# A decoder layer on one core: other places for a rotation, a norm, weight splits and function tables, and an end in halves

## The reference

```
x = x + attention(layernorm(x))        # 16 heads of 32, rotated queries and keys, causal
x = x + cross(layernorm(x), ctx)       # query and key from ctx (512 x 256 per batch), 128 wide
x = x + ffn(layernorm(x))

attention:  q, k, v = split(x @ w_atten.T);  q, k = rope(q), rope(k)
            y = softmax(mask(q k^T / sqrt(32))) v;  return y @ w_proj.T
cross:      energy = (ctx Wq^T + bq)(ctx Wk^T + bk)^T;  return x @ softmax(energy)
ffn:        shared = (silu(x Ws_gate) * (x Ws_up)) Ws_down              # 704 hidden values
            scores = softmax(x W_router);  the two best of 8 experts for each token
            h_e = silu(x We_gate) * (x We_up);  y_e = h_e We_down       # 352 hidden values each
            return sum over the two of score * y_e + shared
```

## Time and profile before

| | us |
|---|---|
| median of three runs | 1010.27 |
| the profiled execution | 1009.63 |
| its span | 1007.6 |
| PE busy in the span | 964.9 (96%) |
| DVE busy | 617.5 (61%) |
| ACT busy | 488.5 (48%) |
| POOL busy | 209.2 (21%) |

### The profile page before, as it was taken

The page is one execution under the profiler, slowest core; times in us unless marked ns, Lnnn a source line. Parts: engine busy times, 40 slices in busy tenths (PEclk is TensorE's granted clock), DMA queues, the critical chain, the costliest instruction groups (busy, mean ns, idle before and its releaser), DMA issues.

```text
span 1007.6 us, 18136 instructions
## 1 busy us (share of the span) xinstructions
PE 964.9 (96%) x6106; PEld 767.1 (76%) x6106; DVE 617.5 (61%) x1625; ACT 488.5 (48%) x1278; POOL 209.2 (21%) x247
## 2 busy tenths in 40 slices
PE   8988899999999999998899999999999999999998
PEld 6457666766767676665667788899889989899997
DVE  5698777867877767768353666524443344434665
ACT  1478765756747566568723331334444344432221
POOL 3222212221112211120000002222232222303342
PEclk9999999999999999999999999999999999999999
DMA  9665854438444473466800211744534542515554
GB/s 242 113 98 74 157 107 64 63 53 244 104 63 64 64 233 65 59 121 206 275 22 21 93 44 53 263 153 166 162 100 140 168 150 85 160 51 157 170 187 144
DMA packets 69834, 124.91 MB, mean 124 GB/s; under 512 B 6336, under 2 KB 22720, under 8 KB 69760
## 3 DMA queue, kind: packets, MB, share of 16 engines
q1 hardware_dynamic: 63296, 104.81, 41.6%
q0 software_dynamic: 5600, 18.35, 6.3%
q10 hardware_dynamic: 864, 0.79, 0.6%
HBM read 70.19 MB, written 28.57 MB: 98 GB/s over the span
## 4 chain that ended last, share of the span: by engine, by line
PE 77%; DVE 11%; issue 3%; DMA 3%; ACT 2%; DVEq 1%; POOL 1%; ACTq 0%; SPq 0%
PE ps L1379 23%; PE ps L1389 12%; PE ps L1139 8%; PE ps L1288 5%; PE ps L1230 5%; PE ps L1191 5%; PE ps L1178 3%; PE ps L1214 3%; PE ps L1164 3%; DVE gu_lo L1703 3%; DMA ks<-rope_a 3%; PE ps L1397 2%; PE ps L1250 2%; PE ps L1080 2%; DVE probs L1552 1%
## 5 line engine op out<-in xcount | busy, mean ns | idle before, releaser
L1552 DVE CUSTOM_DVE_ANT_0 probs<-ps,mask 128x128 f32<-128x128 f32 (+3 forms) x256 | 122.4, 486 | 68.3 <-PE ps L1178 37.6
L885 ACT COPY probsT<-ps 128x128 f32<-128x128 f32 (+3 forms) x256 | 108.7, 426 | 107.6 <-PE ps L1191 66.1
L877 ACT ACTIVATE probs<-probs,nb 128x128 f32<-128x128 f32 (+3 forms) x256 | 146.4, 572 | 24.0 <-DVE nb L1557 23.6
L1178 PE MATMUL ps<-ks,qs 96*128 96x256 f32 (+2 forms) x256 | 128.5, 506 | 13.8 <-DVE mx L1552 10.8
L1191 PE MATMUL ps<-ident,probs 128*128 128x128 f32 x640 | 113.6, 277 | 2.4 <-ACT probsT L885 2.1
L991 ACT ACTIVATE sg<-ps 128x352 f32<-128x352 f32 x69 | 32.1, 465 | 172.5 <-PE ps L1379 172.4
L1837 DVE TENSOR_TENSOR hidden<-sg,ps 128x352 f32<-128x352 f32 x69 | 35.8, 518 | 109.7 <-ACT sg L991 109.7
L1191 PEld LDWEIGHTS ps<-ident,probs 128*128 128x128 f32 x640 | 79.6, 142 | 28.2 <-issue 18.9
L1178 PEld LDWEIGHTS ps<-ks,qs 96*128 96x128 f32 x256 | 49.0, 192 | 51.5 <-DVE mx L1552 23.2
L1389 PE MATMUL ps<-d_hi,h_hi 128*128 128x512 f32 (+1 forms) x207 | 86.8, 419 | 1.3 <-DVE h_lo L1841 1.3
L756 POOL TENSOR_TENSOR rope_a<-rope_a,sin_sb 128x512 f32<-128x512 f32 (+1 forms) x34 | 41.2, 1211 | 225.2 <-DVE rope_a L1534 225.1
(11 more groups left out here) (195 smaller groups left out, 2107.3 us busy)
## 6 DMA issues: line engine op xcount, KB each, us to landing
gu_raw<-in_we SPq DMA_DIRECT2D x10, 1408.0 KB, 6.5
y_d<-y_sb SPq DMA_DIRECT2D x37, 256.0 KB, 3.0
shared_x<-xT_d SPq DMA_DIRECT2D x32, 256.0 KB, 2.7
qs<-rope_b SPq DMA_DIRECT2D x30, 256.0 KB, 5.7
ks<-rope_b SPq DMA_DIRECT2D x30, 256.0 KB, 5.6
d_raw<-in_we SPq DMA_DIRECT2D x10, 512.0 KB, 7.6
attT<-in_wpT SPq DMA_DIRECT2D x4, 1024.0 KB, 8.1
acc<-in_x SPq DMA_DIRECT2D x4, 1024.0 KB, 10.9
```

The lines of the kernel that those rows point to most:

```text
L877: nc.scalar.activation(pr, pr, ACT.Exp, bias=nb[:, n % 2, h:h + 1], scale=SCALE, accum_out=sums[:, n % 2, h:h + 1]).then_inc(exp_done, 1)
L885: nc.scalar.copy(probsT[n % 2][:, h, 0:w], ps[:, T_BANK + h % 2, 0:w]).then_inc(pT_done, 1)
L1178: nc.tensor.matmul(ps[:, S_BANK + h % 2, 0:w], stacks[G % 2][0][:, h, i * P:(i + 1) * P], stacks[G % 2][1][:, h, 0:w], start=True, stop=Tr ...
L1552: nc.vector.tensor_tensor_reduce(probs[n % TT][:, h, 0:w], ps[:, S_BANK + h % 2, 0:w], mask[:, TOKENS - w:], 1.0, LOWEST, ALU.add, ALU.max ...
```

## The change

Places in several tables move, the four parts of an expert's first tile are divided, the place of two dummy SiLUs and of the router's exponential is named, and the last tile ends in halves. The last turn of the hidden values now goes to three banks, of which ACT and DVE each take one third at a time; the last down product goes to two banks of half the columns.

```
-SPLIT_WEIGHTS = (28, 46, 52, 57, 70, 78)
+SPLIT_WEIGHTS = (18, 46, 52, 57, 70, 78)
-OWN_RAW = {..., 15: (1, 5)}
-OWN_SUM = {..., 15: (3, 7)}
+OWN_RAW = {..., 15: (1, 6)}
+OWN_SUM = {..., 15: (3, 8)}
-LN1 = dict(..., turn=(39, 40, 41, 42), copy=(39, 40, 41, 42),
-           low=(40, 41, 42, 43))
-FIRST_LN1 = dict(LN1, ..., scale=(33, 34, 35, 36), turn=(40, 41, 42, 43), copy=(40, 41, 42, 43),
-                 low=(41, 42, 43, 44))
+LN1 = dict(..., turn=(39, 40, 42, 43), copy=(39, 40, 42, 43),
+           low=(40, 41, 43, 44))
+FIRST_LN1 = dict(LN1, ..., scale=(34, 36, 37, 38), turn=(40, 41, 43, 44), copy=(40, 41, 43, 44),
+                 low=(41, 42, 44, 45))
 CROSS = dict(
-    ..., route=(70, 72, 87))
+    ..., route=(70, 72, 87), route_exp=(70,))
 LAST_CROSS = dict(
-    ..., router=(50,), router_copy=(50,), router_turn=(52,), route=(52, 53, 54))
+    ..., router=(50,), router_copy=(51,), router_turn=(52,), route=(53, 55, 56), route_exp=(54,))
-        SPLIT_PLACES = tuple((BATCHES - 1) * PLACES + at for at in (54, 56, 58, 60, 62, 64))
+        SPLIT_PLACES = tuple((BATCHES - 1) * PLACES + at for at in (51, 52, 53, 55, 65, 67))
+        SILU_PLACES = (1, 25)
+        SOONER = 3
+        LAST_HT_BANKS, LAST_Y_BANKS = (HT_BANK, 4, 6), (Y_BANK, 2)
 sp:
                 if t >= 0:
                     sp.wait_ge(acc_link, 2 * (t + 1))
-                    if t == TILES - 1:
-                        sp.wait_ge(shared.y_out, 2 * TILES + 1)
-                    sp.dma_start(out_v[:, t, :], acc[:, t, :]).then_inc(stored, 16)
+                    if t < TILES - 1:
+                        sp.dma_start(out_v[:, t, :], acc[:, t, :]).then_inc(stored, 16)
+            for half, cols in enumerate(HALVES):
+                sp.wait_ge(last_out, half + 1)
+                sp.dma_start(out_v[:, TILES - 1, cols], acc[:, TILES - 1, cols]).then_inc(stored, 16)
 act:
-                    if since == when["route"][0]:
+                    if since in when["route_exp"]:
                         act.wait_ge(r_shift, p + 1)
                         nc.scalar.activation(r_sc[:], r_t[:], ACT.Exp).then_inc(r_exp, 1)
...
                 if j >= 0 and step == 1:
                     turn(shared, j + 1)
-                    if j == 0:
-                        nc.scalar.activation(silu_unused[:], bias_sb[:, 0:1], ACT.Silu)
...
+                if place in SILU_PLACES:
+                    nc.scalar.activation(silu_unused[:], bias_sb[:, 0:1], ACT.Silu)
...
-                split(e + 2, e % 2, range(CC))
+                split(e + 2, e % 2, range(SOONER))
                 silu(routed, lo)
                 turn(routed, lo + 1)
+                split(e + 2, e % 2, range(SOONER, CC))
...
+            act.wait_ge(shared.hT_mm, 2 * TILES)
+            for f in range(NF):
+                nc.scalar.copy(h_hi[:, f, :], ps[:, LAST_HT_BANKS[f], 0:P]).then_inc(last_high, 1)
 pe:
             pe.wait_ge(shared.y_out, 2 * TILES)
-            down(shared, 2 * TILES - 1, 1)
+            for half, cols in enumerate(HALVES):
+                for f, (f0, fn) in enumerate(HCHUNKS):
+                    if half == 0:
+                        pe.wait_ge(last_low, f + 1)
+                    for i, (h, w) in enumerate(((h_hi, d_hi[1]), (h_hi, d_lo[1]), (h_lo, d_hi[1]))):
+                        last = nc.tensor.matmul(ps[:, LAST_Y_BANKS[half], cols], h[0:fn, f, :], w[0:fn, f, cols],
+                                                start=(f == 0 and i == 0), stop=(f == NF - 1 and i == 2))
+                last.then_inc(last_y, 1)
 dve:
-                for i in range(CC):
+                for i in range(SOONER):
                     low_part(e + 2, e % 2, i)
                 gate_by_up(routed, lo)
                 turn(routed, lo + 1)
+                for i in range(SOONER, CC):
+                    low_part(e + 2, e % 2, i)
                 if e == 0:
                     add_shared(TILES - 1)
...
             add_picked(TILES - 1)
-            add_shared(2 * TILES - 1)
+            for half, cols in enumerate(HALVES):
+                dve.wait_ge(last_y, half + 1)
+                at = acc[:, TILES - 1, cols]
+                nc.vector.tensor_tensor(at, at, ps[:, LAST_Y_BANKS[half], cols], ALU.add).then_inc(last_out, 1)
```

More of the change, by code:

```diff
@@ L66 @@
 OWN_KEYS = {1: (3, 7, 7, 7), 2: (0, 2, 3, 3), 3: (-1, 1, 3, 3), 4: (48, 49, 51, 51), 10: (4, 5, 7, 7), 15: (3, 3, 4, 5)}
-OWN_RAW = {1: (5, 8), 2: (0, 5), 3: (0, 7), 4: (49, 55), 10: (2, 7), 15: (1, 5)}
-OWN_SUM = {1: (7, 10), 2: (3, 8), 3: (3, 9), 4: (51, 57), 10: (5, 9), 15: (3, 7)}
+OWN_RAW = {1: (5, 8), 2: (0, 5), 3: (0, 7), 4: (49, 55), 10: (2, 7), 15: (1, 6)}
+OWN_SUM = {1: (7, 10), 2: (3, 8), 3: (3, 9), 4: (51, 57), 10: (5, 9), 15: (3, 8)}
 FIRST_VALUES = ((-1, -1, -1, -1), (5, 7, 7, 9), (9, 10, 10, 10), (10, 10, 12, 13))
 FIRST_VALUE_COPIES = (-1, 10, 11, 14)
-LN1 = dict(stats=(13, 15, 17, 19), variance=(22,), scale=(25, 27, 28, 29), turn=(39, 40, 41, 42), copy=(39, 40, 41, 42),
-           low=(40, 41, 42, 43))
-FIRST_LN1 = dict(LN1, stats=(22, 25, 27, 29), variance=(31,), scale=(33, 34, 35, 36), turn=(40, 41, 42, 43), copy=(40, 41, 42, 43),
-                 low=(41, 42, 43, 44))
+LN1 = dict(stats=(13, 15, 17, 19), variance=(22,), scale=(25, 27, 28, 29), turn=(39, 40, 42, 43), copy=(39, 40, 42, 43),
+           low=(40, 41, 43, 44))
+FIRST_LN1 = dict(LN1, stats=(22, 25, 27, 29), variance=(31,), scale=(34, 36, 37, 38), turn=(40, 41, 43, 44), copy=(40, 41, 43, 44),
+                 low=(41, 42, 44, 45))
 CROSS = dict(
@@ L85 @@
     third_stats=(47, 51, 55, 58), third_variance=(59,), third_scale=(60, 60, 60, 63), third_turn=(61, 61, 62, 65),
[L86 removed]
+    third_copy=(61, 62, 63, 64), store_mixed=(59,), store=(63,), store_turned=(67,), router=(67,), router_copy=(68,), router_turn=(69,), route=(70, 72, 87), route_exp=(70,))
 LAST_CROSS = dict(
@@ L94 @@
     third_stats=(36, 38, 40, 42), third_variance=(43,), third_scale=(45, 45, 46, 46), third_turn=(47, 47, 48, 48),
-    third_copy=(47, 48, 48, 49), store_mixed=(), router=(50,), router_copy=(50,), router_turn=(52,), route=(52, 53, 54))
+    third_copy=(47, 48, 48, 49), store_mixed=(), router=(50,), router_copy=(51,), router_turn=(52,), route=(53, 55, 56), route_exp=(54,))
 def build(nc, x, ctxT, waT, wpT, wqT, wkT, bq, bk, wr, we, cosT, sinT, out):
@@ L493, in build @@
         stored = sem("stored")
+        last_high = sem("last_high")
+        last_low = sem("last_low")
+        last_y = sem("last_y")
+        last_out = sem("last_out")
         waited = sem("waited")
@@ L1065, in _ @@
                     put_routed(total - 1)
-                hidden_high(shared, j)
+                if j < 2 * TILES - 1:
+                    hidden_high(shared, j)
+            act.wait_ge(shared.hT_mm, 2 * TILES)
+            for f in range(NF):
+                nc.scalar.copy(h_hi[:, f, :], ps[:, LAST_HT_BANKS[f], 0:P]).then_inc(last_high, 1)
         @block.tensor
@@ L1482, in _ @@
                     down(shared, j - 1, 1)
-                turn_hidden(shared, j)
-            pe.wait_ge(shared.y_out, 2 * TILES)
-            down(shared, 2 * TILES - 1, 1)
+                if j < 2 * TILES - 1:
+                    turn_hidden(shared, j)
+            pe.wait_ge(shared.h_done, 2 * TILES)
+            for f in range(NF):
+                last = nc.tensor.transpose(ps[:, LAST_HT_BANKS[f], 0:P], hidden[:, f * P:(f + 1) * P], ident[:])
+            last.then_inc(shared.hT_mm, 1)
+            pe.wait_ge(shared.y_out, 2 * TILES)
+            for half, cols in enumerate(HALVES):
[6 more added lines that the diff above has]
+                last.then_inc(last_y, 1)
         @block.vector
@@ L1948, in _ @@
                     add_shared(j - 1)
-                hidden_low(shared, j)
+                if j < 2 * TILES - 1:
+                    hidden_low(shared, j)
+                else:
+                    for f in range(NF):
+                        dve.wait_ge(last_high, f + 1)
+                        nc.vector.tensor_tensor(h_lo[:, f, :], ps[:, LAST_HT_BANKS[f], 0:P], h_hi[:, f, :].bitcast(F32),
+                                                ALU.subtract).then_inc(last_low, 1)
                 t = j - TILES
```

2 lines of the change are left out of this document (1 added, 1 removed).

## The result

The changed kernel took 996.44 us (median of four runs, 995.2 to 997.25), the kernel before 1009.41 in the runs beside them (1008.54 to 1011.1). The ratio is 0.9868, with a 95% interval from 0.9849 to 0.9888: 11 to 15 us faster. The forecast was 997.2, the range 990 to 1003.5. The profiled execution took 997.16, its span 995.15; against the profiled execution of before that is 12.5 us, where the sum said 13.1.

The account below looks back on a forecast made before the run. TensorE (PE) was taken as the bound, busy 964.9 of 1007.6 us, plus its idleness. Terms -0.4 + 1.3 + 1.5 + 2.0 + 3.3 + 5.5 - 0.1 = 13.1 off 1009.63 gave 996.5 profiled, median 997.2; range 990 to 1003.5.

Parts of the forecast that it names:

- The choice of 0.78: First tile of experts 1 to 7: us gained per expert with the fourth low part behind the turn, +5.5 in all.
- Rival 3: Experts pay half, 2.7 for 5.5, as another low part meets POOL's copy; 1000.0 us, chance 0.11.
- 1.75 and the slow stretch's 1.54: Last routing: moving the function tables removes PE's stall and the low clock after it, +3.3 us.
- slow stretch stays: Last routing: lower bound of 1.7 us on the function tables' gain, if the low clock remains.
- a place has a mask of about 0.6 between, so most is covered: Norm of batches 1 and 2: last two turns a place later hide most of PE's 0.87 wait, 0.65 us each.
- the 1.97: Last rotation: us by which the scores awaited at 438.12 come sooner, with scale and mask 230 in DVE's waiting time.
- the two orders behind it: Last rotation: DVE's next scale starts before POOL's low part (place 236 at 442.6) or after (443.5); value +1.5 us.
- rival 4: First FFN weights: ACT stands at place 51 for late weights, making the kernel slower; 1014.5 us for landing at 475, chance 0.04.
- the -0.4: Opening weights and batch 0's norm: loss in us, two later scales pushing the chain to the wait at 92.41 by 0.45.
- such a stall costs itself and some 1.5 us more: PE's stalls: 3 us at granted clock 0.50 hold 1.5 us of full-speed work; four stalls are followed by it.
- Rival 1: Attention's stalls only move on; only tables, experts and end pay, 8.7 us, so 1001.6; chance 0.17.
- Rival 2: Slow stretches all go as every stall before one gets short, 21.7 us, so 988.6; chance 0.15.

Follow-up runs that it names:

- the fourth tile alone: Changed kernel, but in batches 1 and 2 only the next norm's fourth tile is turned a place later, the third stays as before; 995.04 us, again 995.29.
- further edits: Changed kernel with the norm's third tile back, first SiLU and gate product earlier, expert 0's addition and tile 14's picked rows reordered; 994.66 us, again 993.61.
- the norms' kernel: Kernel before with only the opening weight split and the new places of the next norm in all batches; 1009.67 us, ratio 1.0005.
- The parts alone: Kernel before with one part each: experts 1003.37 us, tables 1006.53, rotation 1006.56, weights and end 1006.31, opening split and norms 1009.67.

## Why the prediction was right, and where it was not

*Experts.* This was right in place and size: 5.57 by the marks, 5.6 alone, 5.5 forecast. The choice of 0.78, between the named wait with the second period's excess (0.61) and all of the excess (0.95), is met by 7.28 + 7.07 - 6.84 - 6.69 = 0.82. Rival 3 is out: all 40 low parts of gate and up took 0.88 to 0.90 in the changed kernel, where the earlier trace rows has up to 1.30, and the tokens' low parts kept their 0.69.

*Function tables.* The step "1.75 and the slow stretch's 1.54" was half right. The stall went, 1.8. The low clock is not tied to it: of five profiles with the old routing and the same stall one has it. The bound of 1.7 for "slow stretch stays" was in truth the part's worth. That the marks show 3.34 for 3.3 is luck: the profiled execution of before has a low clock there that the other four lack. The token count's constants did not get late. (The trace has 13 routing instructions ahead of DVE's product, where the prediction counts 12.)

*The norm of batches 1 and 2.* This was wrong: -0.2 for +1.3. The step that failed is "a place has a mask of about 0.6 between, so most is covered": it looked only at who waits for the turn that moves, the fourth tile's. The third tile's low part moved as well, from place 42 to 43, and the mixing product of place 44 waits in the program for it. Moving the fourth tile alone won nearly what had been forecast: 0.59 and 0.61 against the kernel before (19.90 for 20.49 and 20.51), for 0.65 each.

*The last rotation.* The place and the 1.97 were right (2.2). Of the two orders behind it the scale went first, 0.54, and 442.6 was forecast for place 236 in that case; it was 442.82. But the price did not go away, it moved: GpSimd's low part took 1.51, and DVE's copy of the inverse 1.09, where it took 0.23 at this step before. The sum had no term for that copy, although the trace of before shows it beside a low part of GpSimd (59.97 to 61.23): 1.31. First this copy in the kernel before, at its last rotation and at 60; then DVE and GpSimd in the changed kernel:

```profile
441.44 0.23 DVE L1566 COPY inverse<-rsum 128x128 f32<-128x128 f32 x1
```

```profile
60.01 1.31 DVE L1566 COPY inverse<-rsum 128x128 f32<-128x128 f32 x1
```

```profile
439.29 0.54 DVE L1535 TENSOR_SCALAR xn<-acc,norm_mv,norm_rstd 128x512 f32<-128x512 f32 x1
...
439.95 1.09 DVE L1592 COPY inverse<-rsum 128x128 f32<-128x128 f32 x1
```

```profile
439.45 1.51 POOL L771 TENSOR_TENSOR rope_a<-rope_a,rope_b 128x512 fp32r<-128x512 f32 x1 [1.64 <-DVE rope_b L1570]
```

The prediction had the value right, 1.5 for 1.6, and its composition wrong: 0.7 is the order's and 0.9 the clock's, for which the 1.5 had no term.

*First FFN weights.* They gained 1.46 for 2.0, with the low clock in both. The first casts cost 0.46 where 0.2 to 0.3 was said. The last ones held the router's copy as feared only where the clock stayed high: PE waited 0.86 for it in the four profiles with the new places and no low clock there, and 0.34, as before, in the four with one, the changed kernel among them. ACT did not wait for the weights: rival 4 did not come.

*Opening weights and batch 0.* The stall at 73 stayed as forecast. The wait for the DMA of the keys did not get longer (0.19 for 0.39), so the -0.4 did not come; what came cannot be told from nothing. The mark shows 0.86, of which 0.5 is the low clock that was away; the rest is within the spread of the profiles. (DVE's timeline of before is not quite without a gap from 54 us on: it has gaps of 0.29 and 0.24 ahead of 56.44 and 58.25.)

*The end.* It gained 0.37 for -0.1. Of this 0.2 falls behind turn 62, and only that repeats (45.30 to 45.35 in all five profiles with the old end, 45.13 to 45.18 in all six with the halves and no further edits). As said, PE's earlier end did not count; DVE's picked rows set it. The price of two stores did not come: in the same profiles the span ended 2.2 us after the start of the last store's issue, of half the columns, and 2.4 us after that of the whole store.

*The clock.* The step "such a stall costs itself and some 1.5 us more" was the weakest. Two things were wrong in it. First, the price of a low stretch depends on what sets the time where it lies. By pairs of kernels with the same code there, it is 1.5 in the FFN, where PE sets the time (25.24 for 23.72), 0.9 beside the rotation, where DVE does (19.53 for 18.63), 0.4 to 0.9 ahead of place 48, which waits for a DMA, and 0.75 to 1.0 near 477 with the new places (43.89 and 44.12 for 43.14), where PE gets part back by a shorter wait for the router's copy. Second, whether it comes is not settled by the stall alone. Behind the routing's stall of 1.75 it came in one of five profiles. Behind the one at 73, 1.73 to 1.80 long in all thirteen profiles of this study, it came in four of five with the old tables and in none of eight with the new; behind the old rotation's 2.13 in four of five; near 477, with the old places of the weights in all five, with the new places in four of eight, and there with the same outcome in both profiles of each kernel that was run twice. The Trainium skill ("TensorE: Matmul & The Clock Gate", Part 1) says that the gate's windows run freely, so that one kernel can get different outcomes; the five equal stalls of the routing and the single runs (clocks of 0.993 to 0.998 in the norms' kernel) agree with that, the four against none at 73 would not be expected of chance. What decides beside the stall stays open. Over the timed runs the mean granted clock was 0.9945 for before (49 runs) and 0.999 for the changed kernel (9 runs), so part of the clock's gain belongs to the change and not to the one pair. The three low stretches that the profiled pair differs by are worth 0.5 + 0.9 + 1.5 = 2.9 of its 12.5 us by the prices above.

So the total was right, and partly by terms that cancel. Too much was forecast for the norm (1.6) and the weights (0.5), and the start was 0.6 later (not in the second profile of the same kernel, 22.33); too little for place 48 (1.3, of which 0.5 is the clock and 0.4 the cost that did not come) and the end (0.5). The parts alone add up to 5.6 + 2.5 + 2.4 + 2.7 - 0.7 = 12.5 us of medians, the whole to 13.0: within the scatter of the medians, the parts hardly touch one another. Rival 1 (1001.6) fell with the rotation and the weights, which each paid by themselves. Rival 2 (988.6) fell with the stalls at 73 and 477, which stayed; three of its four slow stretches did go in this pair, but for 2.9 us, and the kernel with the fourth tile alone, which has none of the four in either profile, took 995.

## What to carry to other kernels

When an operation moves in a table, look up every wait on its semaphore, not only the wait at the place that shows the stall: the third tile moved along and took the gain back. A stage in which a long job stands ahead of a short one that the bounding engine needs pays its excess period, as often as it comes: count periods, not waits. And price a stall by itself: the low clock behind it in one profile may be missing in the next, and what it costs depends on what bounds the stretch.

## What was not expected of the hardware

Equal stalls of PE ahead of equal matmuls were followed by a granted clock of 0.50 or of 1.00 (one of five, four of five, above), and the low stretch cost between 0.4 and 1.5 us, depending on what bounded the work in it. Where DVE and GpSimd met, both paid: with the new order the scale fell from 1.24 to 0.54, but the copy behind it rose from 0.23 to 1.09 and GpSimd's low part from 1.27 to 1.51.
